# Input projections of three triangle layers: block-diagonal 128-row matmuls in halves of a tile, replaced by 64-row matmuls in pairs of tokens

## What is computed

```
xn    = layer_norm(groupnorm(x))                      # over the 64 channels of a token
left  = (xn @ Wa) * sigmoid(xn @ Wga)                 # layer 3: times mask
right = (xn @ Wb) * sigmoid(xn @ Wgb)
z     = einsum('bikc,bjkc->bijc', left, right)        # one 192x192x192 product per channel
out   = (layer_norm(z) @ Wo) * sigmoid(xn @ Wgo)      # the "output gate"
```

## Time and profile before

| | |
|---|---|
| median of 3 runs | 1985.76 us (1978.09 to 1988.72) |
| profiled execution | 1991.03 us, of which the span of instructions is 1989.2 us |
| busy share of the span | PE 76%, PEld 49%, DVE 82%, ACT 63%, POOL 52% |
| gate stores, ACT's queue | 108 of 256 KB, median 3.1 us from issue to landing |
| matmuls of the projections | 864 records of 128x384 and 864 of 128x256 |
| input stages (from first projection to last product) | 110 to 289 us, 511 to 693 us, 1629 to 1804 us |

### The profile page before, as it was taken

One profiled execution on the slowest core, in us unless ns is written; L12 is line 12 of the kernel. 1 busy time (PEld: TensorE's weight loads), 2 busy tenths in 40 slices (PEclk: granted clock), 3 DMA queues, 4 the chain that ended last, 5 costly groups with the idle time before them and its releaser, 6 DMA issues.

```text
span 1989.2 us, 31133 instructions
## 1 busy us (share of the span) xinstructions
PE 1505.3 (76%) x9710; PEld 975.6 (49%) x9744; DVE 1630.4 (82%) x4038; ACT 1251.1 (63%) x2571; POOL 1028.4 (52%) x730
## 2 busy tenths in 40 slices
PE   5479999798799987981111288888888859998775
PEld 1156668564566685650111124444443437776664
DVE  6899961897999717978999958999989979992488
ACT  2256641896455517974566658777787837772488
POOL 7288830685888406867676501222222268870254
PEclk8789999899899998995555558989899889999869
DMA  6034443676344345771111001111111124435377
GB/s 235 11 85 106 107 103 90 182 198 202 85 107 106 81 122 160 212 201 59 38 42 43 22 0 33 43 43 43 43 44 47 50 80 112 111 91 133 104 233 252
DMA packets 314373, 201.96 MB, mean 102 GB/s; under 512 B 248992, under 2 KB 249312, under 8 KB 314208
## 3 DMA queue, kind: packets, MB, share of 16 engines
q1 hardware_dynamic: 175776, 162.21, 28.0%
q10 hardware_dynamic: 138432, 37.76, 8.1%
HBM read 114.97 MB, written 66.06 MB: 91 GB/s over the span
## 4 chain that ended last, share of the span: by engine, by line
issue 37%; PE 28%; DVE 14%; ACT 9%; POOL 6%; DMA 4%; SPq 0%; ACTq 0%; DVEq 0%; POOLq 0%
PE ps L1088 10%; ACT work L935 7%; PE ps L1093 6%; PE ps L1049 4%; PE ps L1078 4%; PE ps L1168 4%; DMA gate_dram<-work 3%; POOL work L445 3%; POOL work L491 2%; DVE stats L671 2%; ACT work L921 2%; DVE ln_s L687 1%; DVE work L592 1%; DVE pairs L789 1%; DVE pairs L757 1%
## 5 line engine op out<-in xcount | busy, mean ns | idle before, releaser
L485 POOL TENSOR_TENSOR ln_s<-ln_s,half_power 128x8 f32<-128x8 f32 x252 | 417.6, 1657 | 373.3 <-DVE ln_s L680 317.4
L1088 PE MATMUL ps<-work 128*128 128x384 f32 x864 | 319.5, 493 | 3.5 <-ACT work L921 3.5
L1049 PE MATMUL ps<-work,ones 128*128 128x512 f32 x504 | 282.3, 677 | 27.0 <-ACT work L897 17.8
L946 ACT ACTIVATE work<-ps 128x768 f32<-128x768 f32 x216 | 175.1, 811 | 175.0 <-DMA gate_dram<-work 141.2
L935 ACT ACTIVATE work<-pairs,ln_s 128x64 f32<-128x64 f32 x648 | 263.0, 493 | 17.8 <-DVE ln_s L687 17.8
L491 POOL TENSOR_TENSOR work<-pairs,work 128x512 f32<-128x512 f32 x36 | 47.5, 1320 | 372.8 <-DVE pairs L855 372.8
L1093 PE MATMUL ps<-work 128*128 128x256 f32 x864 | 223.4, 381 | 0.0
L477 POOL TENSOR_TENSOR work<-work,gn_rstd 128x512 f32<-128x512 f32 x144 | 185.1, 1286 | 62.4 <-DVE work L636 56.9
L1093 PEld LDWEIGHTS ps<-work 128*128 128x128 f32 x864 | 165.7, 192 | 69.6 <-issue 1.8
L1179 PE MATMUL ps<-ident,pairs 128*64 128x128 bf16 x576 | 38.8, 312 | 201.9 <-DVE pairs L789 201.0
L1088 PEld LDWEIGHTS ps<-work 128*128 128x128 f32 x864 | 156.8, 192 | 70.3 <-ACT work L921 6.9
(11 more groups left out here) (131 smaller groups left out, 3189.5 us busy)
## 6 DMA issues: line engine op xcount, KB each, us to landing
work<-x_mid SPq DMA_DIRECT2D x144, 256.0 KB, 2.7
gate_dram<-work ACTq DMA_DIRECT2D x108, 256.0 KB, 3.1
work<-gate_dram SPq DMA_DIRECT2D x108, 256.0 KB, 3.1
work<-in_x_in SPq DMA_DIRECT2D x72, 256.0 KB, 2.8
work<-x_nat SPq DMA_DIRECT2D x144, 128.0 KB, 3.0
x_mid<-work SPq DMA_DIRECT2D x72, 256.0 KB, 2.1
work<-pairs SPq DMA_DIRECT2D x96, 96.0 KB, 3.0
work<-pairs ACTq DMA_DIRECT2D x96, 96.0 KB, 3.1
```

The costliest lines, as they stand in the source:

```text
L485: pool.tensor_tensor(ln_s[:, b, RSTD, :], ln_s[:, b, VAR, :], half_power[:, 0:U], ALU.pow)\
L946: act.activation(sig[:, b, :].rearrange("p (k g) -> p k g", k=PAIRS)[:, 2 * half:2 * half + 2, :], ps[:, bank:bank + 2, 0:GATES], ACT.Sigm ...
L1049: last = pe.matmul(ps[:, bank, :], ones[:], src[:, b, :], start=first, stop=end, skip_group_check=True)
L1088: last = pe.matmul(ps[:, GATE_BANK[half] + k, 0:GATES], xnT[:, b, (2 * half + k) * P:(2 * half + k + 1) * P], wpair[:, VALUES:VALUES + GAT ...
```

## The change

- `project` works on one pair of tokens. It issues two matmuls of 64 rows x 128 columns of stationary data, one for each token: rows 0 to 63 (even) and 64 to 127 (odd), each with `wfold` directly as moving data, 320 columns, each to a bank of its own.
- Six banks form three pairs of banks, (0,1), (2,3), (6,7), used in turn: pair n of the stage uses `PAIR_BANKS[n % 3]` and waits until the products of pair n-3 are stored.
- There is no `wpair` any more; the output projection's small block-diagonal part is left, as `w_out`. Per layer `pair_weights` made six copies, `output_weights` makes two.
- `gates` is one sigmoid per pair (128x384), `store_pair` one product per pair (128x256; in layer 3 two of 128x128). The semaphores count pairs.
- DVE normalises three tokens in layers 0 and 1 and two in layer 3 (before five and three). ACT's share is issued in two parts, between the sigmoids.
- `store_gate` of tile i-1 comes after the first sigmoid of step i, before it came last in step i.
- The order of the stage lists is changed, as the diff shows.

```diff
-VALUES = 4 * C
-GATES = 6 * C
+VALUES = 2 * C
+GATES = 3 * C
-DVE_TOKENS = {(0, 0): 5, (0, 1): 2, (1, 0): 5, (1, 1): 2, (2, 0): 1, (3, 0): 3, (3, 1): 2}
+DVE_TOKENS = {(0, 0): 3, (0, 1): 2, (1, 0): 3, (1, 1): 2, (2, 0): 1, (3, 0): 2, (3, 1): 2}
-        GATE_BANK = (2, 6)
+        PAIR_BANKS = (0, 2, 6)
-            def pair_weights(q):
+            def output_weights(q):
                 if q == 0:
                     dve.wait_ge(s_fold, 13)
-                    dve.memset(wpair, 0.0).then_inc(w_step, 1)
+                    dve.memset(w_out, 0.0).then_inc(w_step, 1)
...
-                    for lo, src, width in ((0, 0, VALUES // 2), (VALUES, 2 * C, GATES // 2), (2 * PROJ, PROJ, C)):
-                        last = dve.tensor_copy(wpair[rows, lo + h * width:lo + (h + 1) * width], wfold[rows, q, src:src + width])
+                    last = dve.tensor_copy(w_out[rows, C * h:C * h + C], wfold[rows, q, PROJ:PROJ + C])
...
-            def store_pairs(l, half, t, b):
+            def store_pair(l, pair, t, b):
...
-                dve.wait_ge(proj_ready, k + 1)
-                dve.wait_ge(sig_ready, k + 1)
+                dve.wait_ge(sig_ready, n + 1)
                 if l == 3:
-                    for u in range(HALF):
+                    for u in range(2):
...
-                    last = dve.tensor_tensor(dst[:, :, bass.ds(t * U + u0, HALF)].rearrange("p k u -> p u k"),
-                                             values, gates[:, u0:u0 + HALF, 0:2 * C], ALU.mult)
+                    last = dve.tensor_tensor(dst[:, :, bass.ds(t * U + u0, 2)].rearrange("p k u -> p u k"),
+                                             ps[:, bank:bank + 2, 0:VALUES], gates[:, u0:u0 + 2, 0:2 * C], ALU.mult)
...
-                    pipeline(dve, layer_norm(l, 0, xn, 2, [(0, lambda t, b: store_pairs(l, 0, t, b)),
-                                                                (0, lambda t, b: store_pairs(l, 1, t, b))]))
+                    pipeline(dve, [(3, lambda t, b, r: ln_moments(l, 0, t, b, r), RING),
+                                   (0, lambda t, b: store_pair(l, 0, t, b)),
+                                   (2, lambda t, b: ln_shift(l, 0, t, b)),
+                                   (3, lambda t, b: ln_var(l, 0, t, b)),
+                                   (0, lambda t, b: store_pair(l, 1, t, b)),
+                                   (2, lambda t, b, r: normalise(l, 0, xn, t, b, r), RING),
+                                   (0, lambda t, b: store_pair(l, 2, t, b)),
+                                   (0, lambda t, b: store_pair(l, 3, t, b))])
...
+                if pair == 0:
+                    wait_free(act, gate_stored[b], landed(16, tile - 2, b))
+                    wait_free(act, pair_stored, PAIRS * (tile - 1))
+                act.wait_ge(proj_ready, n + 1)
+                bank = PAIR_BANKS[n % 3]
+                act.activation(sig[:, b, 2 * GATES * pair:2 * GATES * (pair + 1)].rearrange("p (e g) -> p e g", e=2),
+                               ps[:, bank:bank + 2, VALUES:PROJ], ACT.Sigmoid).then_inc(sig_ready, 1)
...
                     pipeline(act, [(0, lambda t, b: gates(q, 0, t, b)),
-                                   (1, lambda t, b: evacuate_xnT(tr_base(l, 0) + t, t, b, proj_ready, 2 * (TILES * q + t - 1))),
+                                   (-1, lambda t, b: store_gate(q, t, b)),
+                                   (1, lambda t, b: evacuate_xnT(tr_base(l, 0) + t, t, b, proj_ready, PAIRS * (TILES * q + t - 1))),
                                    (0, lambda t, b: gates(q, 1, t, b)),
-                                   (2, lambda t, b, r: normalise(l, 0, xn, xn_transposed(0), t, b, r), RING),
-                                   (-1, lambda t, b: store_gate(q, t, b))])
+                                   (2, lambda t, b, r: normalise(l, 0, xn, xn_transposed(0), t, b, r, HALF_ONE), RING),
+                                   (0, lambda t, b: gates(q, 2, t, b)),
+                                   (2, lambda t, b, r: normalise(l, 0, xn, xn_transposed(0), t, b, r, HALF_TWO), RING),
+                                   (0, lambda t, b: gates(q, 3, t, b))])
...
+                wait_free(pe, pair_stored, n - 2)
+                for odd in range(2):
+                    rows = slice(C * odd, C * odd + C)
+                    last = pe.matmul(ps[:, PAIR_BANKS[n % 3] + odd, 0:PROJ], xnT[rows, b, pair * P:(pair + 1) * P],
+                                     wfold[rows, q, 0:PROJ], start=True, stop=True)
                 last.then_inc(proj_ready, 1)
...
                     pipeline(pe, [(0, lambda t, b: project(l, 0, t, b)),
+                                  (0, lambda t, b: project(l, 1, t, b)),
                                   (1, lambda t, b, r: transpose_xn(l, 0, t, b, r), RING),
-                                  (0, lambda t, b: project(l, 1, t, b))])
+                                  (0, lambda t, b: project(l, 2, t, b)),
+                                  (0, lambda t, b: project(l, 3, t, b))])
```

More of the change, by code:

```diff
@@ L208, in build @@
          xnT_ready,
-         gates_ready, proj_ready,
+         proj_ready,
          sig_ready,
@@ L234, in build @@
          mlp_out_ready, mres_loaded,
-         s_apart, s_pe_apart) = [sem(f"sem_{k}") for k in range(70)]
+         s_apart, s_pe_apart) = [sem(f"sem_{k}") for k in range(69)]
         x_loaded, gate_stored, xnew_stored, mres_loaded = [
@@ L921, in evacuate_xnT, with normalise @@
                 act.activation(xnT[:, b, :], ps[:, T_BANK + b, :], ACT.Copy, bias=1.0 / ROOT_C).then_inc(xnT_ready, 1)
-            def normalise(l, side, dst, dst_used, t, b, r):
+            HALF_ONE, HALF_TWO, BOTH = (0,), (1,), (0, 1)
+            def normalise(l, side, dst, dst_used, t, b, r, halves=BOTH):
                 n = ln_base(l, side) + t
[L926 to L930, removed]
+                if 0 in halves:
+                    act.wait_ge(shift_step, n + 1)
+                    dst_used(t)
+                    if side:
+                        apart()
+                first = DVE_TOKENS[l, side]
+                middle = (first + U) // 2
+                for u in range(first if 0 in halves else middle, U if 1 in halves else middle):
                     if side == 0:
@@ L936, in normalise, with gates @@
                                           scale=ln_s[:, b, RSTD, u:u + 1], bias=ln_s[:, b, SHIFT, u:u + 1])
[L937 to L946, removed]
-                               ps[:, bank:bank + 2, 0:GATES], ACT.Sigmoid).then_inc(sig_ready, 1)
+                if 1 in halves:
+                    last.then_inc(xn_act, 1)
+            def gates(q, pair, t, b):
+                tile = TILES * q + t
+                n = PAIRS * tile + pair
+                if pair == 0:
+                    wait_free(act, gate_stored[b], landed(16, tile - 2, b))
+                    wait_free(act, pair_stored, PAIRS * (tile - 1))
+                act.wait_ge(proj_ready, n + 1)
+                bank = PAIR_BANKS[n % 3]
+                act.activation(sig[:, b, 2 * GATES * pair:2 * GATES * (pair + 1)].rearrange("p (e g) -> p e g", e=2),
+                               ps[:, bank:bank + 2, VALUES:PROJ], ACT.Sigmoid).then_inc(sig_ready, 1)
             def store_gate(q, t, b):
-                act.wait_ge(sig_ready, 2 * (TILES * q + t + 1))
+                act.wait_ge(sig_ready, PAIRS * (TILES * q + t + 1))
                 act.dma_start(tokens(gate_dram[TILES * q + t]),
@@ L1079, in transpose_xn, with project @@
                 last.then_inc(xnT_psum, 1)
[L1081 to L1084 removed]
+            def project(l, pair, t, b):
+                q = TRIANGLES[l]
+                n = PAIRS * (TILES * q + t) + pair
+                if pair == 0:
                     pe.wait_ge(xnT_ready, tr_base(l, 0) + t + 1)
[L1086 to L1094 removed]
+                wait_free(pe, pair_stored, n - 2)
[3 more added lines that the diff above has]
+                                     wfold[rows, q, 0:PROJ], start=True, stop=True)
                 last.then_inc(proj_ready, 1)
@@ L1168, in project_out @@
                     last = pe.matmul(ps[:, b, k * P:(k + 1) * P], xnT[:, b, k * P:(k + 1) * P],
-                                     wpair[:, 2 * PROJ:], start=True, stop=True)
+                                     w_out, start=True, stop=True)
                 last.then_inc(out_ready, 1)
```

33 lines of the change are left out of this document (10 added, 23 removed).

## The result

The changed kernel takes 1953.95 us (median of 4 runs, 1950.51 to 1954.81), the one before 1986.15 us (median of 4, 1978.09 to 1988.72). The ratio is 0.9841, with a 95% interval of 0.9811 to 0.9872: faster by 1.6%. The prediction was 1936 us, with a range of 1906 to 1988. The span of the profiled execution fell from 1989.2 to 1953.0 us, by 36.2 us where 50 were expected.

A forecast was written before the change was run, and what follows sets the result against it. PE was taken as full, at 4.75 to 4.89 us a tile. Layers 0 and 1 gain 39 us, layer 3 6, weights 5: 50 off 1991.0 is 1941, the median 5 lower: 1936 us, range 1906 to 1988.

The forecast's parts named there:

- Layers 0 and 1: Input stages of these layers: period falls from 4.89 to 4.33 us a tile, 39 us gained together.
- The weights: Before the stages: six weight copies become two, so POOL's power starts 1.7 us earlier in three layers, 5 us.
- The gate store's wait: ACT's 41 us idle in a stretch, for the gate store just issued, ends; the moved store's 0.52 issue is hidden.
- the 1 us of blocking: DVE's tokens held by POOL's large operation; in the new order they run during the power, so it goes away.
- The loop through the engines: Wait loops among PE, ACT and DVE set the period: main loop 4.28 us in layers 0 and 1.
- ACT's branch: Loop through PE, transposes, copy, ACT's sigmoids and tokens: 4.18 us in layers 0 and 1, 4.57 in layer 3.
- The two-tile loop: Longer loop over two tiles through ACT's sigmoids and tokens and DVE's products and moments: 8.65 us, 4.32 a tile.
- the term of layer 3: Layer 3's input stage: period falls from 4.75 to 4.57 us over 35 tiles, 6 us gained.
- POOL alone: Rival: POOL alone bounds, all of the loop being shorter; 1903 to 1915 us, chance 0.10.
- Longer handshakes: Rival: row tiles gain nothing for a lone pair, or handshakes are longer; 4.6 to 4.9, 1958 to 1985 us, chance 0.18.
- The clock: Rival: PE, at work 61%, drops to the 1.2 GHz level; period 5.4, 2053 us, chance 0.09.
- The power blocking tokens: Rival: DVE's three tokens wait about 1 us for POOL's power to end; 2030 us, chance 0.03.

The follow-up runs named there:

- Experiment 5: The no-row-tiles version of the changed kernel, with POOL's `scale` on one token of eight: 1959.84 us (one run).
- Experiment 8: The kernel before with only the token split (3, 3, 2) and the early gate store: 1981.45 us (8 runs), ratio 0.9949.
- experiment 6: The changed kernel without the mask copy; layer 3's products read the mask where it lies: 1945.22 us (one run).
- 7: The changed kernel with DVE's moments and ln_var moved one tile earlier, the moments behind the third pair's product: 1943.34 us, ratio 0.9759.
- 10: The changed kernel with moments and ln_var moved one tile earlier and no mask copy: 1936.10 us, ratio 0.9732.
- 3: The changed kernel with each projection matmul issued twice, same operands and result: 2052.25 us (one run).
- 4: The changed kernel without row tiles: 128-row stationary data against a zero-padded weight matrix: 2020.36 us (one run).
- 2: The changed kernel with ln_shift first in DVE's list, before the moments and the first product: 1942.52 us, ratio 0.9766.
- 9: The changed kernel with the old token split on DVE (5, 5, 3): 2023.98 us (one run).
- 11: The changed kernel with moments and ln_var moved earlier, no mask copy, and three tokens on DVE in layer 3: 1955.79 us, ratio 0.9829.

## Why the prediction was right in its range and wrong in one step

**Right.** Layers 0 and 1 were put at 39 us and gave 38.9 (partly by luck: 4.39 and 4.43 came for 4.33, and layer 1 had stood at 5.02, not at 4.89). The weights were put at 5 and gave 4.9. A pair takes 0.65 and its tail; the sigmoid, product and token durations fit the rows. The gate store's wait went and its issue is hidden. The tokens pass under the power (in 0.73 us), so the 1 us of blocking in the earlier trace rows is gone. Experiment 5 against the changed kernel gives the row tiles (with `scale` cut short, so without the hold): 4.77 without, 4.39 to 4.43 with them in layers 0 and 1, (0.37 + 0.34) x 35 = 25 us; nothing in layer 3. Experiment 8 gives the tokens and the store, (0.15 + 0.24) x 35 = 13.6 us; the two add up to 38.7 of the 38.9.

**The step that failed: "The loop through the engines".** It put layer 3 at 4.57, by ACT's branch through PE and the transposes. The loop that binds there goes nowhere near PE. The edge left out is ACT's first tokens behind ln_shift, which the new list puts behind S3, the moments, the mask copy and S0. The two-tile loop held most of its terms but went on over S1 and DVE's tokens instead; it came near for layers 0 and 1 (4.32 against 4.41), where this loop has two ACT tokens ahead of G2. In layer 3 it has three (0.33 more), two products that are longer (0.12 and 0.09) and a mask copy (0.18): 5.14. So the term of layer 3 was not +6 but -10.1 us. 50 expected and 36.2 measured differ by 13.8, which is those 16 us less the 2.3 at the ends. That it is this loop is shown by experiment 6 (0.2 us out of it gives 0.21) and fits 7 and 10 (the moments, then the mask copy too, out of it, and a held ln_var in it: 4.79 and 4.61); that it isn't PE, by 3 and 4. For layers 0 and 1 the loop is read from the rows, and experiments 2 and 7 (4.36 and 4.22 in layer 0) fit it.

**The rivals.** POOL alone: not in the changed kernel (0.3 us of idle time a tile), but reached in experiment 7's layer 0, at 4.21. Longer handshakes: layer 3's 5.14 lies even above its 4.9, by a loop and not by handshakes. The clock: 1.00 in both windows. The power blocking tokens: it doesn't; the 2030 us given for it stands on the profiled execution, and on the median that the other rivals use it would be 2025. What the prediction said of blocking, that the new order takes it away, holds for the changed kernel's order alone: the margin between the end of the tokens and `scale` is 205.05 - 204.46 = 0.6 us in layer 0, and experiments 3, 9 and 11, layer 1 of experiment 4, and layer 1 of 7 and 10 each use it up.

**Open.** Why the copy of xnT waits 0.17 us longer at about 580 us in layer 1 of experiments 7, 10 and 11. The changed kernel has the clock at 1.00 from 530 to 650 us and keeps its rhythm; in experiment 10 the slow rhythm, with the stretches of half clock that follow it, costs layer 1 some 0.3 us a tile against layer 0, 11 us. Which of the two rhythms layer 1 of experiment 4 takes is settled in its first tiles; by what is open. An order in which neither ln_shift, ln_var nor the tokens can meet a large POOL operation wasn't tried.

## What to carry to other kernels

When a change takes the full engine out of the bound, write down each in-order list of the new code and follow every wait edge once around, the small instructions first: a 0.15 us instruction that stands behind 2 us of others decides the period. Move an instruction on DVE only after looking at what POOL runs at its new time, and ask for the margin, since a loop with a hold in it can have two stable periods, and how a stage starts, or a delay of 0.2 us, can pick the slow one. Then put the work that nobody waits for where its engine waits anyway: that gave here two thirds as much again as the change itself (1.6% to 2.7%).

## What the runs showed of the hardware

- POOL's operations on 128x512 hold some of DVE's instructions till they end: ln_shift took 0.92 instead of 0.15 us, ln_var 0.52 instead of 0.15, three tokens 1.67 to 1.83 instead of 0.73. Not held under them are the moments and the products (0.57 us at 202.73, under L470 of 201.87 to 203.14). The power on 128x8, 1.64 us of POOL, holds no token in any stretch shown here. The Trainium skill ("SBUF — State Buffer", Who interferes with whom) says that a DVE instruction with two SBUF inputs contends with a GpSimd instruction that reads SBUF, that one in a two-port mode contends with GpSimd and one with a single SBUF input otherwise doesn't, and that whoever issues first blocks the other for all of its instruction. The traces agree for ln_shift, moments and products under large operations, and for tokens and ln_var if they are in such a mode, which no trace names; they disagree for the power.
- The same program has two stable periods, by that hold: 4.75 and 5.6 in experiment 4, 4.21 and 5.2 in layer 1 of experiment 7. There 0.17 us of delay on one copy came ahead of the change from one to the other; the half clock came 2.3 us behind it, in experiment 11 29 us.
- The clock fell to 0.51 at 583.5 us in experiment 7. Ahead of it PE was busy 20.08 us of the 23.00 up to 583.0, and 0.94 us of the 2.30 from 581.2 to 583.5. In experiment 11 it was 1.00 over 28.10 us in which PE was busy 18.37, and fell behind them.
